# Gate pass of a graph network kernel: the source-lane one-hots computed on VectorE instead of loaded

## The reference

```
src, dst = (edge_index[0], edge_index[1])
gate = jax.nn.silu(edge_attr @ F1W + F1b) @ F2W + F2b
gate = gate + (emb[atom_z[src]] * (emb[atom_z[dst]] @ adapt)).sum(-1, keepdims=True)
cw = jnp.where(distances < CUT, 0.5 * (jnp.cos(jnp.pi * distances / CUT) + 1.0), 0.0)
mj = node_mult[dst]
msg = gate * h[dst] * (cw * mj)[:, None]
agg = jax.ops.segment_sum(msg, src, num_segments=N)
tot = jnp.clip(jax.ops.segment_sum(mj, src, num_segments=N), 1e-08, None)
h = _ln(h + agg / tot[:, None], gn, bn)
```

## Time and profile before

| | us |
|---|---|
| median of 3 runs | 12576.59 |
| the profiled execution, its own time | 12574.09 |
| its span in the trace | 12572.4 |
| gate pass, first record load to last sum | 3219 to 3857 |
| its part at the full TensorE clock, read in this window | 3310 to 3850 |

### The profile page before, as it was taken

One profiled execution on the slowest core, in us unless ns is written; L12 is line 12 of the kernel. 1 busy time (PEld: TensorE's weight loads), 2 busy tenths in 40 slices (PEclk: granted clock), 3 DMA queues, 4 the chain that ended last, 5 costly groups with the idle time before them and its releaser, 6 DMA issues. The chain is left out here.

```text
span 12572.4 us, 340621 instructions
## 1 busy us (share of the span) xinstructions
PE 9312.7 (74%) x108936; PEld 6748.8 (54%) x108937; DVE 6365.2 (51%) x18244; ACT 3382.7 (27%) x11859; POOL 4625.3 (37%) x6424
## 2 busy tenths in 40 slices
PE   3999867776685994994996897799899995333322
PEld 2777555555674994894895796233233334333322
DVE  6444488888576886886887787200100001222111
ACT  3111133333232662662563564000000010000000
POOL 1777611111562551451452353000000004777755
PEclk9999987777797996996997998899999985555555
DMA  6222266666794992892893795898899961222398
GB/s 269 60 60 60 48 213 222 222 223 220 223 311 124 247 248 70 235 248 76 227 248 104 200 245 140 245 271 265 263 285 288 291 178 29 21 21 21 20 16 16
DMA packets 3258239, 2128.67 MB, mean 169 GB/s; under 512 B 1436065, under 2 KB 2939889, under 8 KB 3258082
## 3 DMA queue, kind: packets, MB, share of 16 engines
q1 hardware_dynamic: 3039426, 1847.30, 51.7%
q0 software_dynamic: 111520, 84.20, 8.3%
q10 hardware_dynamic: 107136, 195.08, 4.3%
HBM read 1657.44 MB, written 467.66 MB: 169 GB/s over the span
## 5 line engine op out<-in xcount | busy, mean ns | idle before, releaser
L1966 POOL DMA_INDIRECT l_row<-H,l_rec x1488 | 1440.3, 968 | 3353.0 <-DMA l_rec<-REC 2779.6
L1755 PE MATMUL p_acc<-p_row,p_feats 128*48 128x512 f32 (+1 forms) x5600 | 2184.5, 553 | 21.0 <-ACT p_feats L1783 17.3
L1127 PE MATMUL l_sums<-l_msg,l_oh 128*128 128x49 f32 x2976 | 720.8, 417 | 1341.6 <-DVEq L2002 1341.6
L1514 POOL TENSOR_TENSOR s_rest<-s_msg 128x196 f32<-128x196 f32 x1488 | 763.2, 513 | 2238.9 <-ACT s_msg L1496 1936.2
L1113 PE MATMUL s_gotd<-m_table_d,s_hot 128*128 x17856 | 1422.6, 205 | 199.1 <-DMA s_hot<-OHT 192.7
L1755 PEld LDWEIGHTS p_acc<-p_row,p_feats 128*48 128x48 f32 x5600 | 683.6, 124 | 1520.7 <-issue 1496.8
L1127 PEld LDWEIGHTS l_sums<-l_msg,l_oh 128*128 128x128 f32 x2976 | 662.5, 328 | 1401.2 <-issue 1401.2
L1496 ACT ACTIVATE s_msg<-s_gotd,s_es 128x49 f32<-128x49 f32 x5952 | 1310.2, 304 | 48.4
L1113 PE MATMUL s_small<-m_table_s,s_hot 128*128 x17856 | 1300.3, 185 | 1.8 <-issue 1.4
L1113 PEld LDWEIGHTS s_gotd<-m_table_d,s_hot 128*128 128x128 bf16 x17856 | 1029.5, 96 | 396.9 <-issue 225.7
L396 POOL DMA_INDIRECT REC<-rec,place x800 | 949.4, 1187 | 317.7 <-issue 214.0
(11 more groups left out here) (373 smaller groups left out, 19599.3 us busy)
## 6 DMA issues: line engine op xcount, KB each, us to landing
p_row<-ADJ SPq DMA_DIRECT2D x400, 1600.0 KB
s_hot<-OHT SPq DMA_DIRECT2D x1488, 384.0 KB, 3.8
s_rec<-REC SPq DMA_DIRECT2D x1488, 98.0 KB, 3.6
OHT<-a_turned ACTq DMA_DIRECT2D x372, 384.0 KB, 2.4
ADJ<-a_acc SPq DMA_DIRECT2D x1116, 128.0 KB, 1.7
g_hot<-OHT SPq DMA_DIRECT2D x372, 384.0 KB, 4.1
REC<-fill SPq DMA_DIRECT2D x124, 624.0 KB, 10.3
ADJ<-a_acc ACTq DMA_DIRECT2D x372, 128.0 KB, 1.8
```

Of the source, the lines that this page charges most:

```text
L1127: return nc.tensor.matmul(flat[:, bass.ds(at, SW)], hot, msg, start=False, stop=False, skip_group_check=True)
L1514: nc.gpsimd.tensor_tensor(rest[:, b % KEPT].rearrange("p g w -> p (g w)"), msg[:, b % KEPT].rearrange("p g w -> p (g w)"), upper(msg[:, b ...
L1755: last = nc.tensor.matmul(acc[0:H, q, 0:n * P], feats[:, u], block_row[:, u, cols], start=first and u == 0, stop=False, skip_group_check=True)
L1966: nc.gpsimd.indirect_dma_start(out=row[:, b, j], out_offset=None, in_=table, in_offset=bass.IndirectOffsetOnAxis(ap=rec[:, b, j, GIDX - NO ...
```

## The change

1. A new constant `iota_bf`: 0 to 127 along the free axis, in bf16 (one more GpSimd instruction at the start of the program).
2. The `hot` load fetches kinds 0 and 1 only: 256 KB a group instead of 384, in 512 pieces of 512 bytes instead of 128 of 3072.
3. A DVE stage `sources`, last in the DVE turn: for each of the four tiles one `tensor_scalar` compares `iota_bf` with the tile's column of source lanes and writes a 128x128 bf16 one-hot into a ring of 6 (OWN). It waits for the group's loads and for s_agg of group n-6, and signals s_own.
4. PE's `add` takes these as weights, and waits for s_own as well.
5. SP's `rec` load waits for s_own as well as for s_msg.

```diff
-            for name in ("iota",):
+            for name in ("iota", "iota_bf"):
...
     SLOTS = 12
     KEPT = 4
+    OWN = 6
...
-        hot = room.sb("hot", [P, SLOTS, G, HOT, P], BF16)
+        hot = room.sb("hot", [P, SLOTS, G, 2, P], BF16)
+        own = room.sb("own", [P, OWN, G, P], BF16)
...
                     if past(n, SLOTS):
                         sp.wait_ge(s_msg, n - (SLOTS - 1))
+                        sp.wait_ge(s_own, n - (SLOTS - 1))
                     sp.dma_start(rec[:, b], numbers(mem, n, CW, RW)).then_inc(s_in[b], 16)
...
-                    sp.dma_start(hot[:, b].rearrange("p g k c -> p (g k c)"),
-                                 mem["OHT"][bass.ds(n, 1)].rearrange("g p w -> p (g w)")).then_inc(s_in[b], 16)
+                    sp.dma_start(hot[:, b].rearrange("p g k c -> p g (k c)"),
+                                 mem["OHT"][bass.ds(n, 1)].rearrange("g p (j w) -> p (g j) w", j=G)[:, :, 0:2 * P]
+                                 ).then_inc(s_in[b], 16)
...
                 def add(n, b, lap):
 
+                    pe.wait_ge(s_own, n + 1)
                     pe.wait_ge(s_split, n + 1)
...
-                            last = nc.tensor.matmul(sums[b % 2][:, 0:SW], hot[:, b, j, 2], thirds[k],
+                            last = nc.tensor.matmul(sums[b % 2][:, 0:SW], own[:, b % OWN, j], thirds[k],
...
+                def sources(n, b, lap):
+                    dve.wait_ge(s_in[b], 32 * lap + 32)
+                    if past(n, OWN):
+                        dve.wait_ge(s_agg, n - (OWN - 1))
+                    for j in range(G):
+                        last = v.tensor_scalar(own[:, b % OWN, j], mem["iota_bf"][:], rec[:, b, j, SL - CW:SL - CW + 1],
+                                               None, ALU.is_equal)
+                    last.then_inc(s_own, 1)
...
-                laps(dve, [(crossed, 0), (shifted, 1), (shifts, 0), (times_h, 1), (cut_off, 0)], SLOTS)
+                laps(dve, [(crossed, 0), (shifted, 1), (shifts, 0), (times_h, 1), (cut_off, 0), (sources, 0)], SLOTS)
```

More of the change, by code:

```diff
@@ L534, in _ @@
         def _(dve):
-            dve.wait_ge(s_diff, 2)
+            dve.wait_ge(s_diff, 3)
             for name in ("ident_bf", "ident_hf", "ident"):
@@ L770, in scratch @@
                             ("apart", [P, P], BF16), ("upper", [P, P], F32), ("lower", [P, P], F32),
-                            ("iota", [P, P], F32), ("cap", [P, G], F32)):
+                            ("iota", [P, P], F32), ("iota_bf", [P, P], BF16), ("cap", [P, G], F32)):
         mem[name] = nc.alloc_sbuf_tensor("m_" + name, shape, dt)
@@ L1155, in gate_pass @@
         s_in = [room.sem(f"s_in{b}") for b in range(SLOTS)]
-        s_got, s_ej, s_cross, s_shift, s_scaled, s_gated, s_msg, s_rest, s_split, s_agg, s_part, s_dve = (
+        s_got, s_ej, s_cross, s_shift, s_scaled, s_gated, s_msg, s_rest, s_split, s_agg, s_part, s_dve, s_own = (
             room.sem(n) for n in ("s_got", "s_ej", "s_cross", "s_shift", "s_scaled", "s_gated", "s_msg", "s_rest",
-                                  "s_split", "s_agg", "s_part", "s_dve"))
+                                  "s_split", "s_agg", "s_part", "s_dve", "s_own"))
         got = [room.ps(f"got{b}", [P, G, 113]) for b in range(KEPT)]
```

## The result

| | before | after |
|---|---|---|
| median of 4 runs each, us | 12574.72 | 12774.58 |
| lowest to highest, us | 12571.80 to 12577.59 | 12766.66 to 12778.00 |
| span of the profiled execution, us | 12572.4 | 12773.3 |

The ratio after to before is 1.0158, interval 1.0145 to 1.0171: the change makes the kernel about 200 us slower. The two profiled spans differ by 200.9.

What follows compares the result with a forecast made beforehand. PE's own queue was taken to set the gate pass's 1.62 us turn. DVE's 1.64 + 2 x 0.31 = 2.26 us would replace it: 333 turns, +213 us on 12574.1, forecast 12790; 8-in-10 range 12625 to 12905.

Steps and rivals of the forecast that it cites:

- Load, nothing gained: Gate pass loads: a third fewer one-hot bytes gain nothing, since gathers have them 9 us early; SP's longer issue is hidden.
- PE's third wait, 0: PE's add: s_own shares an EVENT_SEMAPHORE with the wait already there, costing 0; bounds 0 and +19 us.
- DVE's own work, 4 x 0.16 = 0.64 a turn: DVE's gate-pass turn: four new tensor_scalar at 0.16 us each, bounds 0.40 to 0.80, raise 1.00 us to 1.64.
- Two waits for POOL, 2 x 0.31 = 0.62: DVE's turn: the second new instruction waits for g_rest, the fourth for g_least, 0.31 us each; turn 2.26 us.
- The early turns, no cost: Gate pass until about 3300 us: turns of 2.61 us, longer than DVE's 2.26, keep their length.
- The rule of the Trainium skill: DVE and GpSimd share an SBUF port pair: whoever comes second, including a 2-port tensor_scalar, waits for the whole instruction.
- The clock falls: Gate pass: PE, less busy, gets 1.2 GHz and turns of 2.61 us; 12855 to 12920 us, chance 0.17.
- No port wait, DVE's turn: Gate pass: tensor_scalar never waits for POOL, g_gated meets g_least; turn 1.84 us, 12620 to 12720, chance 0.24.
- Hidden: Gate pass: new instructions cost 0.10 us each without POOL waits; turn 1.60 within PE's 1.62, time 12577, chance 0.10.
- Faster: Gate pass: relieved DMA queues shorten turns to PE's best, 1.56 us; 12518 to 12557 us, chance 0.04.

Runs made afterwards that it cites:

- load_only: The kernel before with only the new load of two one-hot kinds in 512 pieces, so other numbers are summed: 12806.42 us, ratio 1.0006.
- old_load: The changed kernel with the old load of all three one-hot kinds: 12989.67 us, ratio 1.0147 to the kernel before.
- third_wait: The kernel before with one more wait, on s_msg, in PE's add: 12586.68 us, ratio 1.0004.
- pool_small: The changed kernel with POOL's two instructions on 4 numbers a partition instead of 196: 12812.32 us, ratio 1.0010 to the kernel before.
- lanes_psum: The changed kernel with the tensor_scalar reading lane numbers as f32 from PSUM, not bf16 from SBUF: 12729.38 us, ratio 1.0119 to the kernel before.
- one_compare: The changed kernel with one tensor_tensor on 128x512, both inputs broadcast, instead of four tensor_scalar: 12628.10 us, ratio 1.0039 to the kernel before.
- two_tiles: The changed kernel with one-hots made for two of the four tiles, each used twice: 12682.90 us, ratio 1.0082 to the kernel before.
- spread: The changed kernel with its four tensor_scalar placed after g_cross (one), g_shift (two) and g_scaled (one): 12873.13 us, ratio 1.0059 to the kernel before.

## Why the prediction was right

Forecast 12790, slower; measured 12774.6. Mechanism and place were as forecast. Term by term:

- *Load, nothing gained.* Right, shown by load_only from one side and old_load from the other. A DMA share of 1.01 was no bound: with 0.93 in load_only the turn is the same.
- *PE's third wait, 0.* Within its bounds (0 and +19): third_wait has +6.5 us, with an interval that includes 0, and one more instruction in 60 of 372 groups, which the reading from ACT's line missed. In the changed kernel it decides nothing, since DVE sets the turn.
- *DVE's own work, 4 x 0.16 = 0.64 a turn.* Measured 0.65, shown by pool_small alone, where nothing else is in the way. The value lay between bounds of 0.10 and 0.20; the nearest row (a constant instead of a column, 0.14 in the earlier trace rows) was the right neighbour. That 0.16 came out to the hundredth is partly luck, since no row isolated the column. The slack had a flaw that the sum didn't use: DVE had not 0.42 but 1.62 - 1.00 = 0.62 us to spare. Of a turn, 0.12 went into the waits of g_gated (471 ns for 347) and 0.08 was the end of g_scaled, which no follower overlapped.
- *Two waits for POOL, 2 x 0.31 = 0.62.* They are there, at the second and the fourth of each turn as forecast, but worth 0.535 together, 0.27 each. This is the term that was mis-sized. I had the hold from g_gated (0.38 us behind POOL's start). A tensor_scalar goes on sooner: the fourth one in the shown turn starts at 3506.43, behind a g_least of 3506.37, and ends at 3506.93; less its own 0.24 it began in earnest at 3506.69, 0.32 behind POOL's start. The forecast turn was 2.26 and the measured one 2.187; over 332 groups that is 24 us too much.
- *The early turns, no cost.* A little wrong: the first 40 groups, by ACT's copies of the sums, take 94.6 us instead of 87.0, +8. With the 6 us behind the pass this made up for more than half of the 24, so the time came out nearer than the turn did; that part is luck.
- *The rule of the Trainium skill ("SBUF — State Buffer", section "Who interferes with whom")* was to be tested for tensor_scalar, which no row of before showed. The runs agree with it: 0.50 instead of 0.24 us with the operands in SBUF, no stretching with the input in PSUM (lanes_psum), and POOL as the one that waits when it comes second (one_compare). Its "whole instruction" is longer than what I see: a wait ends 0.32 (tensor_scalar) to 0.38 us (g_gated) after the start of a POOL instruction recorded as 0.51.

The rivals:

- *The clock falls.* It did, to 0.77 on average over the pass, but the price that I gave this was wrong. I had 2.61 us for a turn at the low clock, as in the early stretch, and so 12855 and more. In the changed kernel a turn is as long at either level: of the same 280 turns the 69 wholly at 0.50 take DVE 2.18 us on average, the 119 wholly at 1.00 take it 2.20. DVE never idles, and PE keeps up with it even at the low clock: in the stretch at 0.50 shown above its first gathers of two turns start at 3509.89 and 3512.07, 2.18 apart. Over all turns it waits 0.3 us for its sums (96.0 us in 316 turns). The 2.61 us belonged to the early stretch and not to the clock alone; what else makes those turns longer, no run shows.
- *No port wait, DVE's turn* (the prediction once calls it the third rival). Refuted: no tensor_scalar would be long, and g_gated would be. It is the reverse in the changed kernel. As worked out, this rival assumed that g_gated meets g_least; that meeting came back in two_tiles.
- *Hidden* failed on the waits. The 94 ns that the Trainium skill ("VectorE: DVE Perf Modes", the errata table for TRN2 and the perf-mode tiers) gives for this size, in a row that the page itself says comes out too short, is below the 162 ns between starts in pool_small and in the changed kernel; with it the own work would have been 0.38 us instead of 0.65. Its waits alone would still have made the kernel slower, as two_tiles (0.32 us of work) shows.
- *Faster* is out with load_only, whose interval begins at 0.9996: the relief of the queues is worth at most 0.04%.

## What to carry to other kernels

Before work is moved to VectorE because it has slack, look at where GpSimd's instructions fall: DVE's old work took 1.00 us of a turn of 1.62, so 0.65 us more should have cost 0.03 us a turn, and cost 0.57, since short SBUF instructions in a row were placed exactly where two GpSimd instructions follow a signal. Moving the same four instructions within the turn took more than half of that away, and one instruction without gaps took more. And a full DMA share means little as long as the data are there turns before they are read: look at who waits for the transfer, not at how full the queues are.

## What the runs showed of the hardware

- A tensor_scalar of 128 bf16 numbers against a column takes 0.162 us start to start; four of them on 512 numbers (0.65 us) cost nearly what one tensor_tensor with two broadcast inputs costs (0.60). With f32 input from PSUM it is 0.26.
- Between two DVE instructions in a row, a POOL instruction that is ready gets SBUF; a tensor_scalar behind it waits 0.27 us. Inside one long DVE instruction it gets nothing and waits for the end (0.89 to 0.97 us instead of 0.51).
- An event-semaphore instruction holds two waits, at 51 ns on PE; a third wait needed one more in 60 of 372 groups and made PE's turn 1.642 us for 1.622 (third_wait).
- The granted clock fell from 1.00 to 0.76 in the changed kernel, where TensorE waited at its sums 203 times in 316 turns, and this cost nothing here, since VectorE set the turn. Waiting in most turns does not by itself bring the clock down: in two_tiles TensorE waits for DVE before its gathers in 171 of 212 turns, and the clock is 0.98. It was 0.97 in spread (turn 1.83 us), 0.98 in two_tiles (1.89) and 0.89 in lanes_psum (2.03). What decides it, no run shows.
